# A shared expert's down products taken block by block, and 25 products that nobody reads at a scan's entry

## The chip, the cores and the metric

One NeuronCore of a Trainium2 chip runs the whole program in one launch. The metric is the device time of that launch in microseconds (us), the median over runs. Engines are called as the profile calls them: PE is TensorE (PEld its weight loads), DVE VectorE, ACT ScalarE, POOL GpSimd, SP the sync engine, whose queue (SPq) issues most DMAs.

## The reference, cut to what matters

16 sequences of 113 tokens (36 image patches and 77 text tokens) of width 256 go through an attention layer, a mixture-of-experts layer, a selective-scan (Mamba-like) layer and a fake-quantised gated FFN, each behind a layernorm and with a residual. The change touches the second and the entry of the third:

```python
# mixture of experts; x_ is (1808, 256)
idx = argmax(x_ @ router.T)                      # one of 8 experts for each token
y  = down_e( silu(x_ @ gate_e.T) * (x_ @ up_e.T) )          # by the chosen expert e
ys = silu(x_ @ w_gate_s.T) * (x_ @ w_up_s.T) @ w_down_s.T   # shared expert, 512 hidden units
out = y + ys
...
# selective scan; x = layernorm(h)
x_in, res = split(x @ in_proj_w.T + in_proj_b)
xc = silu(causal_conv4(x_in) + conv_b)
delta, Bp, Cp = split(xc @ x_proj_w.T + x_proj_b);  delta = softplus(delta @ dt_proj_w.T + dt_proj_b)
```

## The kernel before

Each engine has its own hand-written program; the order on an engine is the order of the code, and engines meet only by semaphores (`wait_ge`, `then_inc`). Loops (`Fori`) hold most repeated steps. PSUM is one tensor `ps` of 8 banks. Float32 products on PE show as two records each in the profile, bf16 products as one: 16 float32 products are "x32" there.

**Shared expert** (`pe_shared`, PE). Four groups of four sequences (452 tokens). In a group, for each of four blocks m of 128 hidden units, PE makes two gate and two up products (L1507) into banks 3 and 4 or 5 and 6. ACT takes the silu of the gate (L615), DVE multiplies it with up into `s_hT` block m (L1028, signals `sh_ready`). Then come the group's 16 down products (L1516): sequence by sequence, and within a sequence over the four blocks; the output of two sequences fills a bank (0 or 1), and `sdown_ps` tells DVE to add it to `resid` (L1032). All of them stand behind one wait for block 3. After the first block of group 0, `pe_counts` counts the router's choices (L1494, L1495). DVE turns them into slots, and POOL scatters all tokens into `slots_in` in DRAM, sorted by expert, with 16 indirect DMAs (L514).

**The experts' opening turns** (`pe_first_turns`, L1531). When the scatter is done, SP loads the first two tiles of 128 sorted tokens (`load_tile`, L390), and PE transposes them (four products, into banks 2 and 7). This stands in group 3, ahead of the gate and up products of its last block:

```python
            group(3, between=(HT - 1, pe_first_turns))
```

**Experts** (`pe_experts`). 22 tiles: gate and up (L1547), turning of the hidden block (L1566), turning of the tile two ahead (L1538), down (L1559). SP issues the loads of tile 2 and later only behind `sp.wait_ge(sdown_ps, 8)`, the last down product of the shared expert, and behind the loads of the scan's weights into the place of the shared expert's weights (`sh_w`), since all are on one queue. SP issues the FFN's gate and up weights right behind tiles 0 and 1.

**Scan entry** (`pe_ssm`, PE). After the last expert tile, DVE quantises a weight, PE turns it (L1610), ACT copies it (L665, `wqT_ready`); the experts' answers are gathered by DMA, DVE adds them to `resid` and takes statistics for sequences 0 and 1, then normalises these into `xn3` (L1226). PE turns them (`turn`, L1670), projects (`project_in`, L1680, two halves of 8 records), convolves (`convolve`, L1690), projects again (`project_x`, L1699; `project_dt`, L1706). ACT stands between: x3T (L718), pads (L729), silus (L740, L745) with a table load before and after, then `act_rstd` for the other 14 sequences (L544, L546), the projections (L754, L756) and softplus (L763 on). DVE adds the answers of those 14 sequences meanwhile (L1210, L1212) and works out their variance (L853), on which L544 waits. Then `step(0)` of the scan begins.

Of the kernel before, what the change touches and what calls it, by code (L numbers as in the profile page):

```python
# [17 lines left out]
P = 128  # L18
B, IMG, TXT, D = 16, 36, 77, 256
# [11 lines left out]
HT = HID // P  # L31
# [5 lines left out]
UP, GATE, DOWN, EW = 0, KT * HID, 2 * KT * HID, 2 * KT * HID + HT * D  # L37
# [15 lines left out]
AT_NORMALISE, AT_TURN, AT_IN, AT_PAD = 4, 5, 6, 7  # L53
OPENING = 1
AT_SKIP = (3, 4)
FIRST_SEQS, OTHER_SEQS = slice(0, GB), slice(GB, B)
BUT_ONE_SEQS, ONE_SEQ = slice(0, B - 1), slice(B - 1, B)
ROUTER_BANKS = (0, 1, 3, 4)
# [40 lines left out]
def build(nc, a, out):  # L99
    ctx = ExitStack()  # L100
    with ctx:
        def sb(name, shape, dt=F32):
            return ctx.enter_context(nc.sbuf_tensor(name, shape, dt))

        def sem(name):
            return ctx.enter_context(nc.semaphore(name))

        ps = ctx.enter_context(nc.psum_tensor("ps", [P, 8, 512], F32))
# [74 lines left out]
        sh_w = sb("sh_w", [P, EW])  # L183
# [66 lines left out]
        pick = pl.take((32 * P // 2,), 96).bitcast(BF16).rearrange("p (j m) -> p j m", j=32)  # L250
# [71 lines left out]
        sgate_ps, sup_ps, sgate_ready, sh_ready = sem("sgate_ps"), sem("sup_ps"), sem("sgate_ready"), sem("sh_ready")  # L322
        sdown_ps, sresid_ready = sem("sdown_ps"), sem("sresid_ready")
# [1166 lines left out]
        def pe_counts(pe):  # L1490

            pe.wait_ge(chosen_ready, 1)
            flat = chosenb[:, :, :].rearrange("p b e -> p (b e)")
            pe.matmul(ps[0:S, 2, 0:B * EXPERTS], upperb[:, :], flat, start=True, stop=True).then_inc(counts_ps, 1)  # L1494
            pe.matmul(ps[0:S, 7, 0:B * EXPERTS], onesb[:, :], flat, start=True, stop=True).then_inc(counts_ps, 1)  # L1495

        def pe_shared(pe):
            pe.wait_ge(xT2_ready, B)
            def group(g, between=None):
                for m in range(HT):  # L1500
                    if between is not None and between[0] == m:
                        between[1](pe)
                    par = m % 2
                    pe.wait_ge(sh_ready, g * HT + m + 1)
                    for bank, at, done in ((3 + 2 * par, GATE, sgate_ps), (4 + 2 * par, UP, sup_ps)):
                        for k in range(KT):
                            last = pe.matmul(ps[:, bank, 0:4 * S], sh_w[:, at + k * HID + m * P:at + k * HID + (m + 1) * P],  # L1507
                                             xT2[:, k, bass.ds(g * 4 * S, 4 * S)], start=k == 0, stop=k == KT - 1)
                        last.then_inc(done, 1)
                pe.wait_ge(sh_ready, g * HT + HT + 2)  # L1510
                for pair in range(2):
                    pe.wait_ge(sresid_ready, 2 * g + pair + 1)
                    for r in range(2):
                        for m in range(HT):
                            b = 2 * pair + r
                            last = pe.matmul(ps[0:S, pair, r * D:(r + 1) * D], s_hT[:, m, b * S:(b + 1) * S],  # L1516
                                             sh_w[:, DOWN + m * D:DOWN + (m + 1) * D], start=m == 0, stop=m == HT - 1,
                                             skip_group_check=True)
                    last.then_inc(sdown_ps, 1)

            group(0, between=(1, pe_counts))
            with pe.Fori(1, 3) as g:
                group(g)
            group(3, between=(HT - 1, pe_first_turns))

        def pe_first_turns(pe):
            pe.wait_ge(slots_ready, 1)
            for j, bank in enumerate(FIRST_TURNS):
                pe.wait_ge(xg_in[j], 16)
                for k in range(KT):  # L1530
                    last = pe.transpose(ps[:, bank, k * ETILE:(k + 1) * ETILE], xg[j][:, k * P:(k + 1) * P], ident)  # L1531
                last.then_inc(xgT_ps, 1)
# [128 lines left out]
                last.then_inc(fdown_ps, 1)  # L1661

        def pe_ssm(pe):
            def turn(g, first=False):
                pe.wait_ge(xn3_ready, GB * g + GB)
                if not first:
                    pe.wait_ge(proj_ready, 4 * g)
                for k in range(KT):
                    for r in range(GB):
                        last = pe.transpose(ps[:, 0, k * N + r * S:k * N + (r + 1) * S], xn3[r][:, k * P:(k + 1) * P], ident[0:S, 0:S])  # L1670
                last.then_inc(x3T_ps, 1)

            def project_in(g, par, half, first=False):

                pe.wait_ge(x3T_ready, g + 1)
                if not first:
                    pe.wait_ge(softplus_ready, g)
                for m in range(half * KT, half * KT + KT):
                    for k in range(KT):
                        last = pe.matmul(ps[:, 1 - m // KT, m % KT * N:(m % KT + 1) * N], in_w[:, k, m * P:(m + 1) * P], x3T[par][:, k, :],  # L1680
                                         start=k == 0, stop=k == KT - 1, skip_group_check=True)
                    if m % KT == KT - 1:
                        last.then_inc((xin_ps, res_ps)[m // KT], 1)

            def convolve(g):

                pe.wait_ge(xpad_ready, KT * g + KT)
                for m in range(KT):
                    for t in range(TAPS):
                        last = pe.matmul(ps[:, 1, m * N:(m + 1) * N], conv_diag[:, m, t, :], xpad[:, m, :, t:t + S],  # L1690
                                         start=t == 0, stop=t == TAPS - 1, skip_group_check=True)
                last.then_inc(conv_ps, 1)

            def project_x(g, par):
                pe.wait_ge(xc_ready, KT * g + KT)
                pe.wait_ge(res_ready, KT * g + KT)
                for w, rows, at in ((rank_w, RANK, 0), (bc_w, 96, N)):
                    for k in range(KT):
                        last = pe.matmul(ps[0:rows, 0, at:at + N], w[:, k, :], xc[par][:, k, :], start=k == 0, stop=k == KT - 1,  # L1699
                                         skip_group_check=True)  # L1700
                last.then_inc(proj_ps, 1)

            def project_dt(g):
                pe.wait_ge(proj_ready, 4 * g + 1)
                for m in range(KT):
                    last = pe.matmul(ps[:, 1, m * N:(m + 1) * N], dt_w[:, m * P:(m + 1) * P], rankT, start=True, stop=True, skip_group_check=True)  # L1706
                last.then_inc(dt_ps, 1)
# [31 lines left out]
            def skip(g, par, r):  # L1739
                if r == 0:  # L1740
                    pe.matmul(ps[0:S, 7, 0:GB * D].rearrange("p (b d) -> p b d", b=GB), ones2[:, 0:S],
                              outskip_b.unsqueeze(1).broadcast_to([2, GB, D]), start=True, stop=False, skip_group_check=True)
                for k in range(KT):
                    pe.matmul(ps[0:S, 7, r * D:(r + 1) * D], x3T[par][:, k, r * S:(r + 1) * S], skip_w[:, k, :], start=False,
                              stop=False, skip_group_check=True)
# [9 lines left out]
            def step(g, par, more=True, before=True, turn_next=True):  # L1755
                for c in range(CHUNKS):
# [22 lines left out]
                    if more and c == AT_RANK:  # L1779
                        project_x(g + 1, 1 - par)  # L1780
                    if c in AT_SKIP:
                        if before:
                            pe.wait_ge(resid3_ready, g)
                        skip(g, par, AT_SKIP.index(c))

            pe.wait_ge(diag_done, KT * (TAPS + 1))
            pe.wait_ge(pick_done, 1)
            pe.wait_ge(wqT_ready, 2 + 2 * FT + FT // 2)
            turn(0, first=True)
            for half in range(2):  # L1790
                project_in(0, 0, half, first=True)
            convolve(0)
            project_x(0, 0)
            project_dt(0)
            turn(1)
            spread(0, 0, 0)
            step(0, 0, before=False)
# [9 lines left out]
        @block.tensor  # L1807
        def _(pe):
            pe_tokens(pe)
            pe_attention(pe)  # L1810
            pe_router(pe)
            pe_shared(pe)
            pe_experts(pe)
            pe_weights_down(pe)
            pe_ssm(pe)
            pe_ffn(pe)
# [81 lines left out]
```

## Time and profile before

| | |
|---|---|
| time, median of 3 runs | 817.71 us (815.85 to 823.74) |
| the profiled execution | 817.4 us, its span 815.5 us |
| busy share of the span | PE 83%, PEld 56%, DVE 62%, ACT 47%, POOL 42% |
| mean granted clock of PE | 0.911 of 2.4 GHz |

The span runs from the first to the last instruction of the profile; 1.9 us lie around it. Times of rows count from the span's start. A granted clock of 1.00 is 2.4 GHz, one of 0.50 is 1.2 GHz. The stages that matter here: the shared expert from 205.6 to 293.5 us, the experts to 432.7, the scan's entry to about 463, the scan itself to about 745.

### The profile page before, as it was taken

What the parts mean: (1) busy time and instruction counts of PE and PEld (TensorE: products, weight loads), DVE (VectorE), ACT (ScalarE), POOL (GpSimd) and SP (SyncE); (2) the same over time, 40 slices, a digit from 0 to 9 for tenths busy, and PEclk for the clock granted to TensorE, in tenths of its full rate; (3) what the DMA queues carried; (4) which work ended last, traced back from release to release, by engine and by line L of the source; (5) the groups of instructions that cost most, each with busy time, mean ns of one, the idle gap of its engine ahead of it and who ended that gap; (6) DMA issues with size and microseconds to landing.
All of it is one profiled execution on the core that took longest, in us unless ns stands there. A gap on an engine that the chain in (4) does not pass through costs nothing. (4 is left out here: it accounts for less than half of the span.)

```text
span 815.5 us, 11659 instructions
## 1 busy us (share of the span) xinstructions
PE 677.0 (83%) x3648; PEld 453.4 (56%) x3649; DVE 503.9 (62%) x899; ACT 380.6 (47%) x843; POOL 345.5 (42%) x328
## 2 busy tenths in 40 slices
PE   7599999998999879999994878797887886733886
PEld 5478888876555446666663655455454552301444
DVE  1556666665412114444215768988988988995687
ACT  0366666763322103233222665665755755211965
POOL 0011211110357203232231168878879789540336
PEclk9899999997999998999997799999999997856799
DMA  9993000000021331111114201202202202000003
GB/s 243 311 426 126 0 0 0 0 2 1 5 41 27 113 107 40 46 41 50 40 39 105 92 31 62 92 2 92 92 0 92 92 1 92 1 0 0 1 1 92
DMA packets 28837, 52.89 MB, mean 65 GB/s; under 512 B 10976, under 2 KB 23684, under 8 KB 26628
## 3 DMA queue, kind: packets, MB, share of 16 engines
q1 hardware_dynamic: 20067, 47.62, 17.3%
q0 software_dynamic: 8736, 4.85, 2.4%
q8 instruction: 18, 0.29, 0.1%
q14 instruction: 16, 0.12, 0.0%
HBM read 42.75 MB, written 9.60 MB: 64 GB/s over the span
## 5 line engine op out<-in xcount | busy, mean ns | idle before, releaser
L483 POOL TENSOR_TENSOR arena<-arena 128x904 f32<-128x904 f32 x64 | 124.7, 1952 | 59.3 <-DVE arena L1251 53.0
L1251 DVE TENSOR_TENSOR_SCAN arena<-ps,arena 128x452 f32<-128x452 f32 x128 | 133.5, 1085 | 6.7 <-ACT ps L777 2.1
L777 ACT ACTIVATE ps<-arena,sh_w 128x448 f32<-128x448 f32 x128 | 80.3, 635 | 107.7 <-DVE arena L1251 106.8
L1730 PE MATMUL ps<-arena,const 128*128 128x452 f32 x112 | 63.3, 650 | 41.2 <-POOL arena L487 41.2
L1547 PE MATMUL ps<-arena,work 128*128 x176 | 83.5, 599 | 0.0
L557 ACT ACTIVATE work<-ps,work 113x113 f32<-113x113 f32 x256 | 66.8, 387 | 32.2 <-DVE work L908 32.2
L1241 DVE TENSOR_TENSOR arena<-arena,ps 128x904 f32<-128x904 f32 x64 | 69.2, 1082 | 11.0 <-PE ps L1717 10.8
L431 POOL TENSOR_TENSOR xT<-work 128x452 f32<-128x452 f32 x16 | 15.1, 944 | 142.2 <-DVE work L897 142.2
L530 POOL DMA_INDIRECT answers_e<-work,slot_token x22 | 23.7, 1075 | 110.0 <-DVE work L1046 110.0
L487 POOL TENSOR_TENSOR arena<-arena 128x452 f32<-128x452 f32 x56 | 64.0, 1143 | 4.4
L514 POOL DMA_INDIRECT slots_in<-xn,slot x16 | 37.9, 2366 | 56.0 <-issue 56.0
L1507 PE MATMUL ps<-xT,sh_w 128*128 128x452 f32 (+1 forms) x128 | 53.0, 572 | 0.0
L1730 PEld LDWEIGHTS ps<-arena,const 128*128 128x128 f32 x112 | 19.2, 207 | 53.2 <-POOL arena L487 53.1
L1042 DVE TENSOR_TENSOR work<-ps,work 128x512 f32<-128x512 f32 x22 | 15.2, 691 | 52.2 <-PE ps L1547 52.2
L1559 PE MATMUL ps<-arena,work 128*128 x176 | 43.5, 391 | 0.8 <-ACT work L628 0.8
L1547 PEld LDWEIGHTS ps<-arena,work 128*128 128x128 f32 x176 | 31.2, 192 | 22.9 <-issue 22.3
L908 DVE TENSOR_REDUCE work<-ps 113x4 f32<-113x452 f32 x64 | 35.8, 621 | 11.5 <-PE ps L1378 11.5
L1507 PEld LDWEIGHTS ps<-xT,sh_w 128*128 128x128 f32 x128 | 25.6, 202 | 24.0 <-issue 23.6
L1680 PE MATMUL ps<-arena,sh_w 128*128 128x226 f32 x128 | 37.9, 457 | 0.7 <-ACT arena L718 0.7
L1357 PE MATMUL ps<-work 128*128 128x113 f32 x256 | 35.6, 297 | 2.3 <-ACT work L551 1.7
L624 ACT ACTIVATE work<-ps 128x512 f32<-128x512 f32 x22 | 13.1, 597 | 52.3 <-PE ps L1547 52.3
L615 ACT ACTIVATE work<-ps 128x452 f32<-128x452 f32 x16 | 8.8, 548 | 60.3 <-PE ps L1507 60.3
(243 smaller groups left out, 1394.6 us busy)
## 6 DMA issues: line engine op xcount, KB each, us to landing
arena<-c_rows SPq DMA_DIRECT2D x8, 1808.0 KB, 6.4
arena<-in_ex_w SPq DMA_DIRECT2D x8, 1536.0 KB, 23.9
slots_in<-work SPq DMA_DIRECT2D x1, 2827.0 KB, 23.5
work<-slots_in SPq DMA_DIRECT2D x22, 128.5 KB, 2.0
xn<-answers_e SPq DMA_DIRECT2D x4, 448.0 KB
out<-resid SPq DMA_DIRECT2D x8, 224.0 KB
arena<-in_patches SPq DMA_DIRECT2D x3, 576.0 KB, 6.3
sh_w<-in_sh_w SPq DMA_DIRECT2D x1, 1536.0 KB, 11.5
```

What stands on the lines that cost most here:

```text
L483: pool.tensor_tensor(read[kp], state[kp], c_all[par][:, 2 * c:2 * c + 2, :].unsqueeze(2).broadcast_to([P, 2, KT, N]), ALU.mult)\
L487: pool.tensor_tensor(read[kp][:, 0], read[kp][:, 0], read[kp][:, 1], ALU.add).then_inc(pair_ready, 1)
L514: pool.indirect_dma_start(slots_in, bass.IndirectOffsetOnAxis(ap=slot[:, b:b + 1], axis=0), xn2_named[:, b, :], None).then_inc(scattered, 16)
L557: last = act.activation(probs[:, r, j], ps[0:S, 3 + r, j * S:(j + 1) * S], ACT.Exp, bias=negmax[:, h:h + 1])
L777: act.activation(decay_ps(n)[:, :, 1:], delta[par].rearrange("p k (b s) -> p (k b) s", b=GB)[:, :, 1:], ACT.Exp, scale=a_neg[:, 2 * c + n: ...
L1241: dve.tensor_tensor(drive[kp], dx[par].unsqueeze(1).broadcast_to([P, 2, KT, N]), ps[:, 2 + kp, 0:2 * N].rearrange("p (n s) -> p n s", n=2) ...
L1251: dve.tensor_tensor_scan(state[kp][:, n].rearrange("p k s -> p (k s)"), decay_ps(n).rearrange("p q s -> p (q s)"), drive[kp][:, n].rearran ...
L1507: last = pe.matmul(ps[:, bank, 0:4 * S], sh_w[:, at + k * HID + m * P:at + k * HID + (m + 1) * P], xT2[:, k, bass.ds(g * 4 * S, 4 * S)], s ...
L1547: last = pe.matmul(ps[:, bank, :], xgT[par][:, k, :], arena[:, bass.ds(e * EW + at + k * HID, HID)], start=k == 0, stop=k == KT - 1)
L1559: last = pe.matmul(ps[:, 6, 0:D], e_hT[:, m, :], arena[:, bass.ds(e * EW + DOWN + m * D, D)], start=m == 0, stop=m == HT - 1)
L1680: last = pe.matmul(ps[:, 1 - m // KT, m % KT * N:(m % KT + 1) * N], in_w[:, k, m * P:(m + 1) * P], x3T[par][:, k, :], start=k == 0, stop=k ...
L1730: pe.matmul(ps[:, 6, 0:KT * N], ident, read[kp][:, 0].rearrange("p k s -> p (k s)"), start=False, stop=False, skip_group_check=True).then_ ...
```

## The change

In the shared expert's groups the loop over blocks m is now the outer one of the down products: the products of block 0 for all four sequences, then block 1, and so on, each block behind its own wait for `sh_ready`, so that only block 3's products wait for block 3. Four sums are open at once, in four regions of banks 0 and 1; `start` is set on the first product of each bank alone. Both `sdown_ps` signals come within the last block. The opening turns go from before the last block of gate and up products to before the last block of down products in group 3. At the scan's entry PE gets `stay_busy(n)`: n bf16 products of 128 x 384 into bank 7, which nobody reads: 19 ahead of the first turn, 2 behind it, 4 behind the convolution.

```diff
+FILL = (19, 2, 4)
...
         def pe_shared(pe):
             pe.wait_ge(xT2_ready, B)
-            def group(g, between=None):
+            def group(g, counts=False, turns=False):
                 for m in range(HT):
-                    if between is not None and between[0] == m:
-                        between[1](pe)
+                    if counts and m == 1:
+                        pe_counts(pe)
...
-                pe.wait_ge(sh_ready, g * HT + HT + 2)
-                for pair in range(2):
-                    pe.wait_ge(sresid_ready, 2 * g + pair + 1)
-                    for r in range(2):
-                        for m in range(HT):
+                for m in range(HT):
+                    if turns and m == HT - 1:
+                        pe_first_turns(pe)
+                    pe.wait_ge(sh_ready, g * HT + m + 3)
+                    for pair in range(2):
+                        if m == 0:
+                            pe.wait_ge(sresid_ready, 2 * g + pair + 1)
+                        for r in range(2):
                             b = 2 * pair + r
                             last = pe.matmul(ps[0:S, pair, r * D:(r + 1) * D], s_hT[:, m, b * S:(b + 1) * S],
-                                             sh_w[:, DOWN + m * D:DOWN + (m + 1) * D], start=m == 0, stop=m == HT - 1,
+                                             sh_w[:, DOWN + m * D:DOWN + (m + 1) * D], start=m == 0 and r == 0, stop=m == HT - 1,
                                              skip_group_check=True)
-                    last.then_inc(sdown_ps, 1)
-
-            group(0, between=(1, pe_counts))
+                        if m == HT - 1:
+                            last.then_inc(sdown_ps, 1)
+
+            group(0, counts=True)
             with pe.Fori(1, 3) as g:
                 group(g)
-            group(3, between=(HT - 1, pe_first_turns))
+            group(3, turns=True)
...
         def pe_ssm(pe):
+            def stay_busy(products):
+                for _ in range(products):
+                    pe.matmul(ps[:, 7, 0:3 * P], pick[:, 0, :], pick[:, 0:3, :], start=True, stop=True)
...
             pe.wait_ge(wqT_ready, 2 + 2 * FT + FT // 2)
+            stay_busy(FILL[0])
             turn(0, first=True)
+            stay_busy(FILL[1])
             for half in range(2):
                 project_in(0, 0, half, first=True)
             convolve(0)
+            stay_busy(FILL[2])
             project_x(0, 0)
```

How PE's program moves in the last group of the shared expert. Before (L1507 gate and up, L1531 the opening turns, L1516 down):

```order
127 L1507 MATMUL ps<-xT,sh_w 128x452 x12
128 L1531 MATMUL ps<-const,work 128x128 x4
129 L1507 MATMUL ps<-xT,sh_w 128x452 x4
130 L1516 MATMUL ps<-sh_w,work 113x256 x16
131 L1570 TENSOR_LOAD tile_expert
```

After, where L1508 is gate and up, L1536 the turns, L1520 down:

```order
130 L1508 MATMUL ps<-xT,sh_w 128x452 x16
131 L1520 MATMUL ps<-sh_w,work 113x256 x12
132 L1536 MATMUL ps<-const,work 128x128 x4
133 L1520 MATMUL ps<-sh_w,work 113x256 x4
134 L1575 TENSOR_LOAD tile_expert
```

The turns have moved behind four more gate and up products and twelve down products (one row is one product here, not one record).

PE's program at the scan's entry, before (L1610 the last weight's turns, L1670 turn, L1680 project_in, L1690 convolve, L1699 project_x, L1706 project_dt):

```order
408 L1610 MATMUL ps<-const,work 64x128 x2
409 L1670 MATMUL ps<-const,arena 128x113 x4
410 L1680 MATMUL ps<-arena,sh_w 128x226 x8
411 L1690 MATMUL ps<-arena,xT 128x226 x8
412 L1699 MATMUL ps<-arena,sh_w 64x226 x2
413 L1699 MATMUL ps<-arena,sh_w 96x226 x2
414 L1706 MATMUL ps<-arena,sh_w 128x226 x2
```

After (L1671 the products nobody reads, L1679 turn, L1689 project_in, L1699 convolve, L1708 project_x):

```order
411 L1615 MATMUL ps<-const,work 64x128 x2
412 L1671 MATMUL ps<-xT 128x384 x19
413 L1679 MATMUL ps<-const,arena 128x113 x4
414 L1671 MATMUL ps<-xT 128x384 x2
415 L1689 MATMUL ps<-arena,sh_w 128x226 x8
416 L1699 MATMUL ps<-arena,xT 128x226 x8
417 L1671 MATMUL ps<-xT 128x384 x4
418 L1708 MATMUL ps<-arena,sh_w 64x226 x2
```

Nothing else moves on PE, and no instruction of another engine changes.

## Rows read from the trace of the kernel before

**Rows 1.** Windows: stretch in us, length, busy of each engine, PEclk, DMA share, GB/s.

```profile
313.00:432.00 119.00, 118.21 (x468) 73.41 (x467) 45.37 (x112) 34.19 (x72) 35.79 (x79) 1.00 0.14 43
...
281.00:283.00 2.00, 2.00 (x4) 0.81 (x3) 0.00 (x0) 0.00 (x0) 0.60 (x3) 0.50 1.01 332
440.00:445.00 5.00, 0.00 (x0) 0.00 (x0) 3.41 (x17) 1.95 (x4) 0.00 (x0) 0.50 0.99 239
448.00:450.00 2.00, 2.00 (x7) 1.76 (x7) 1.90 (x7) 0.00 (x0) 0.00 (x0) 0.50 0.00 0
```

**Rows 2.** Timeline of PE, shared expert: start us, us, what [idle before <-releaser].

```profile
220.65 7.16 PE L1516 MATMUL ps<-sh_w,work 128*113 128x256 f32 x32 [0.79 <-DVE work L1028]
227.64 12.30 PE L1507 MATMUL ps<-xT,sh_w 128*128 x32
240.81 7.16 PE L1516 MATMUL ps<-sh_w,work 128*113 128x256 f32 x32 [0.87 <-DVE work L1028]
...
267.97 9.26 PE L1507 MATMUL ps<-xT,sh_w 128*128 128x452 f32 x24
280.20 0.81 PE L1531 MATMUL ps<-const,work 128*128 128x128 f32 x4 [2.96 <-DMA work<-slots_in]
280.80 4.88 PE L1507 MATMUL ps<-xT,sh_w 128*128 128x452 f32 x8
286.47 7.16 PE L1516 MATMUL ps<-sh_w,work 128*113 128x256 f32 x32 [0.79 <-DVE work L1028]
293.46 5.31 PE L1547 MATMUL ps<-arena,work 128*128 x12
...
306.74 0.69 PE L1538 MATMUL ps<-const,work 128*128 128x128 f32 x2 [5.80 <-DMA work<-slots_in]
```

**Rows 3.** Instructions of line L1507: duration ns min/median/max, first and last start.

```profile
L1507 PE MATMUL ps<-xT,sh_w x128: 542/542/1059, 205.6 to 285.1; 128*128 128x452 f32 x64, 128*128 x64
```

**Rows 4.** Timeline of SP's queue, from the first tile load to the third.

```profile
278.02 0.80 SPq L390 DMA_DIRECT2D work<-slots_in  x2
...
293.66 0.35 SPq L400 DMA_DIRECT2D sh_w<-in_in_w  x1
...
301.82 24.22 SPq L390 DMA_DIRECT2D work<-slots_in  x5
```

**Rows 5.** Timeline of all engines at the scan's entry.

```profile
439.61 0.65 ACT L665 ACTIVATE dq<-ps 128x256 bf16<-128x256 f32 x2 [0.20 <-PE ps L1610]
...
445.49 0.98 PE L1670 MATMUL ps<-const,arena 113*128 113x113 f32 x4 [5.91 <-DVE arena L1226]
...
447.17 5.41 PE L1680 MATMUL ps<-arena,sh_w 128*128 128x226 f32 x16 [0.70 <-ACT arena L718]
...
452.41 3.22 PE L1690 MATMUL ps<-arena,xT 128*128 128x226 f32 x16
...
455.67 0.79 ACT L745 ACTIVATE arena<-ps,sh_w 128x226 f32<-128x226 f32 x2 [2.19 <-PE ps L1690]
...
456.51 1.92 PE L1699 MATMUL ps<-arena,sh_w 128*64 128x226 f32 x8 [0.88 <-ACT arena L745]
...
457.16 0.17 DVE L853 SCALAR_TENSOR_TENSOR lnt<-lnt 113x14 f32<-113x14 f32 x1
...
457.77 0.21 ACT L544 ACTIVATE lnt<-lnt 113x14 f32<-113x14 f32 x1
...
458.46 0.45 ACT L754 ACTIVATE arena<-ps,sh_w 64x226 f32<-64x226 f32 x1 [0.23 <-PE ps L1699]
...
460.02 0.79 ACT L763 ACTIVATE arena<-ps,sh_w 128x226 f32<-128x226 f32 x2
460.04 0.58 PE L1670 MATMUL ps<-const,arena 113*128 113x113 f32 x4
```

**Rows 6.** Timeline: the second convolution, in the scan's first step.

```profile
471.97 4.96 PE L1690 MATMUL ps<-arena,xT 128*128 128x226 f32 x16 [2.65 <-ACT arena L729]
```

**Rows 7.** Timeline of PE: products that nobody reads, in the FFN stage, as they stand before.

```profile
783.47 2.47 PE L1616 MATMUL ps<-arena,identb 128*128 128x452 bf16 x12 [1.70 <-DVE arena L1151]
```

## The prediction

> **What bounds the kernel now.** I read the page first (PE busy for 83% of the span), then windows by stage, then the timelines of the two places that the change touches, and the chain of waits for what follows them. In the experts' stage PE is busy for 118.2 of 119 us at full clock [rows 1]: PE alone sets its length, so whatever time it starts earlier it ends earlier, provided that its data come earlier too. Ahead of it lies the shared expert, also PE's: in PE's timeline [rows 2] the reader is to see two kinds of holes. Each group's down products wait for DVE's product of block 3 (0.79 to 0.87 us), and the opening turns wait 2.96 us for the tiles that SP loads when the scatter is done. Behind that second hole the eight gate and up records from 280.80 take 4.88 us, while 24 of them took 9.26 before: the granted clock is 0.50 from 281 to 283 [rows 1], the 1.2 GHz level, after PE stood still for 3 us. At the scan's entry PE stands for 5.91 us until DVE has normalised the first two sequences [rows 5], with the clock at 0.50 through the wait and into the projections [rows 1].
>
> **The waits for block 3.** How much do they cost from start to start? Group 1: down at 220.65, gate and up at 227.64, down at 240.81. The 32 gate and up records take 12.30 us, the last of them 0.54 [rows 3], so 31 steps take 11.76, a step 0.379 and 32 steps 12.14; from 227.64 to 240.81 are 13.17, so 1.03 us are lost. Group 2 repeats it (1.03); in groups 0 and 3 the idle row is 0.79 in place of 0.87, so 0.95 each. Together 3.96 us. In the new order the first down products need block 0, whose `s_hT` was ready three blocks ago, and block 3's products come after 24 records at (227.64 - 220.65) / 32 = 0.218 us, 5.2 us; block 3 was late by 1 us. No new wait takes the place of the old. The three more waits in a group are on counts long reached: nothing. `sdown_ps` of the first pair comes 2 us or more later than before, but DVE then has over 5 us until the next group's first product, and PE asks for the sums (`sresid_ready`) 12 us later: hidden. Gain 3.96.
>
> **The opening turns.** PE's start of group 3 comes earlier by the three waits before it, 3.0 us: 264.95. Then 32 gate and up records, 12.14, to 277.1, and 24 down records, 5.2, to 282.3. The tiles were there at 280.1: the scatter hangs on the router's counts in group 0 (unchanged place) and on its own DMAs, and SP issues the loads at 278.02 [rows 4], so this time stays. PE arrives 2.2 us after them and waits for nothing. What goes: the hole, from the due next start (267.97 + 9.26 - 0.54 + 0.38 = 277.07) to 280.20, 3.13 us; and the low clock behind it: seven steps from 280.80 to the last start at 285.14 take 4.34 in place of 7 x 0.379 = 2.65, so 1.69; the turns themselves, 0.2 or nothing, I take 0.1. Gain 4.9. Is ACT late with the copies of the turned tiles? They are due at 284.6, when PE begins the experts; the turns end at 282.8 and eight down records (1.75) still stand between: no.
>
> Sum: 3.96 + 4.9 = 8.9 us at the end of the shared expert, 293.46 to about 284.6. **Does it stay?** The next hole is at 306.74, where PE waits 5.80 us for tile 2 [rows 2]. That load does not hang on the scatter: SP gets past its wait for the last down product at 293.66, issues sixteen loads of scan weights, reaches tile 2 at 301.82, and it lands by 306.7 [rows 4]. So this chain, 13.3 us, starts with PE's last down product and moves with it. The FFN weights that SP issues right behind tiles 0 and 1 (1.57 MB) fill the DMA engines (share 1.01 at 332 GB/s from 281 to 283, [rows 1]); at that rate they take 4.7 us and end by 285 or 286, and scan weights will now be issued from 284.8. They overlap by 1.5 us at most: the cost is between nothing and 1.5. I take nothing, since SP spends eight us on issuing the scan weights, time enough for what is left over to drain. Then the experts' stage moves whole.
>
> **The scan's entry.** The 19 products start when ACT's last weight copy is done, 440.3 [rows 5], and the turn's data come at 445.4: 5.1 us to fill. Twelve of the FFN's bf16 products of 452 columns take 2.47 us [rows 7], less the last's 0.35 that is 0.193 a step, 0.164 for 384 columns at full clock and twice that, 0.33, at the low one. So 19 take 3.1 us (all full) to 6.2 (all low): end between 443.4 and 446.5, against 445.4. As the projections rose to full clock some 4 us after PE began at 447.17, a switch midway is likely, and the fill ends within half a us of the data. Gain from the clock: the turn takes 0.58 in place of 0.98, and 16 records of projection 3.22 (the convolution's pace) in place of 5.41 [rows 5]: 0.4 + 2.2 = 2.6 us for PE, less at most 1.1 if the fill overruns. The two products behind the turn (0.3) lie in a wait of 0.70, the four behind the convolution (0.65) in one of 0.88.
>
> But **what is late next?** After its silus ACT must do `act_rstd` for the other 14 sequences, which needs DVE's L853, done at 457.33; before, L544 began at 457.77, just when the table load after the silus was done. DVE's chain of additions does not feel PE's clock. So L544 comes 0.4 earlier, no more. L754 then waits no longer for the projection (0.23), which makes 0.6. But PE, done at some 456, stands for over 2 us until L754, and the clock may fall there again: then project_dt (four records) takes 0.7 longer and L763, at 460.02 before, gains nothing. Of 2.6 us between -0.2 and 0.6 come through; I take 0.4.
>
> **Sum.** 3.96 + 4.9 + 0.4 = 9.3 us from a profiled 817.4, whose span was 815.5. The profiled execution stands 0.3 below the median, so from 817.7: 808.4.
>
> **A rule that speaks against it.** The down products before filled one region of one bank at a time; now every pair of records goes to another of four regions in two banks. The trace shows the gate and up products switching banks every four records at an even 0.379 step and a granted clock of 1.00. The Trainium skill (TensorE: Matmul & The Clock Gate, section "A second HAM failure mode: psum-queue depth-cycling") tells of a kernel whose cycling through PSUM banks left small gaps in PE's work, so that its clock swung between the levels. No run here shows that yet; it is the mechanism of the last rival below.
>
> **The rivals.**
> (a) *The clock is kinder than in this profile.* In the scan's first step the convolution [rows 6] takes 4.96 us, 1.74 over its full-clock 3.22, and the chain of waits runs through it. With PE's work shifted, the clock may stand high there: 817.7 - 9.3 - 1.7 = 806.7. For it: here the fall came just as that convolution began. Against: the median holds other executions with other luck. Chance 0.13.
> (b) *Part is given back between 285 and 320 us*: the overlap of weight loads delays tile 2 by 1.5, or the clock is low for one more stretch of 1.7 behind that wait (it falls there already). 9.3 - 1.6 = 7.7: 810.0. With both, 811.6. Chance 0.17.
> (c) *The fill overruns*, at the low clock all through: the turn is 1.1 late, and the projections cold as before. The silus then end 1.1 later, with the table load behind them, and L544 begins at 458.9 instead of 457.77. 8.9 - 1.1 = 7.8: 809.9. Chance 0.08.
> (d) *The change does not do what it says*: the shared expert ends earlier, but tile 2 does not come earlier (the queue's transfers, not PE, set it), and PE's wait at 306.74 grows by what was won. Then only the entry counts: 817.3. Against it stands that SP issued nothing from 280 to 293.66. Chance 0.07.
> (e) *Slower*: the down products, cycling over two banks, leave gaps, and the clock falls in them. At the low level a record takes 0.22 us more. 42 of the 128 records at the low level eat 9.3 us; from there on it is slower. With all 128, 28 us: 817.7 - 9.3 + 28 = 836. Chance 0.05.
>
> **How the numbers follow.** The forecast has 0.50: 808.4, by itself 806.5 to 810.5, since the entry's term is worth 0.6 at most and runs of the same kernel differ by a few us. The bound that a measurement can tell, 1%, is 8.2 us here: faster means below 809.5. Of the forecast three quarters lie below it, 0.38, with (a) 0.13 and parts of (b) and (c), 0.07: 0.58. Slower is (e), 0.05 (all of it taken over 1%). The rest, 0.37, is the same. The range 805.0 to 812.0 holds the forecast, (a), (b) and (c), 0.88 by name and some 0.8 with what I have not thought of.
>
> **What the profile after would show.** Right, if: no idle row over 0.3 us stands ahead of L1520, the turns (L1536) have no wait for a DMA, granted clock 1.00 from 212 to 300; the experts' first products (L1552) start at 284 to 285; the wait for tile 2 is again 5 to 6 us, and its load is issued 8 us after the last down product; the fill's 19 products end within 1 us of the turn, project_in takes 3.3 to 4 us; L544 directly follows L853, and L763 stands no more than 0.7 us nearer to the entry's start than before. Wrong, if: the tiles land later than PE's arrival, tile 2's wait grows, down records take over 0.22 a step, or the entry gives all 2.6 us, which would mean that ACT's wait for DVE was not the bound.

## The result, and the profile after

The changed kernel takes 807.91 us (median of 4 runs, 804.52 to 809.96), the kernel before beside it 816.78 (4 runs, 815.21 to 823.74): a ratio of 0.9872, 95% interval 0.9835 to 0.9908, so 8.9 us less. The forecast was 808.4, its range 805.0 to 812.0. The same kernel measured once more (e11, below) took 810.26 beside 817.30, 7.0 us less, ratio 0.9908. The profiled execution of the changed kernel took 809.96 with a span of 808.2 and stands at the upper end of its runs, so between the two traces only 7.3 us of span are to be found, not 8.9.

PE's timeline of the shared expert, after (columns as in [rows 2]):

```profile
205.61 5.76 PE L1508 MATMUL ps<-xT,sh_w 128*128 128x452 f32 x8
211.21 0.22 PE L1495 MATMUL ps<-chosenb,upperb 113*113 113x128 bf16 x1
...
220.48 7.07 PE L1520 MATMUL ps<-sh_w,work 128*113 128x256 f32 x32
227.38 12.30 PE L1508 MATMUL ps<-xT,sh_w 128*128 x32
239.52 7.07 PE L1520 MATMUL ps<-sh_w,work 128*113 128x256 f32 x32
...
265.46 12.30 PE L1508 MATMUL ps<-xT,sh_w 128*128 128x452 f32 x32
277.60 5.34 PE L1520 MATMUL ps<-sh_w,work 128*113 128x256 f32 x24
282.78 0.60 PE L1536 MATMUL ps<-const,work 128*128 128x128 f32 x4
283.21 1.89 PE L1520 MATMUL ps<-sh_w,work 128*113 128x256 f32 x8
284.94 5.31 PE L1552 MATMUL ps<-arena,work 128*128 x12
...
298.45 0.69 PE L1543 MATMUL ps<-const,work 128*128 128x128 f32 x2 [6.04 <-DMA work<-slots_in]
```

No row from 220.48 to 284.94 has idle time in brackets: the waits for block 3 are gone. From 227.38 to 239.52 are 12.14 us: 32 steps of 0.379 and nothing else, where [rows 2] had 13.17. The turns stand inside the down products and wait for no DMA. The windows answer to [rows 1]: the stretch from 281 to 283, in which the granted clock was 0.50, is at 1.00.

```profile
212.00:284.00 72.00, 72.00 (x247) 44.80 (x246) 17.61 (x38) 17.87 (x24) 39.09 (x22) 1.00 0.20 40
281.00:283.00 2.00, 2.00 (x12) 1.62 (x12) 0.00 (x0) 0.00 (x0) 1.20 (x6) 1.00 0.54 148
```

SP's queue, after, answers to [rows 4]: from the first scan weight behind the last down product (285.13) to tile 2 (293.28) it takes 8.15 us, as before (293.66 to 301.82).

```profile
279.22 0.80 SPq L391 DMA_DIRECT2D work<-slots_in  x2
...
285.13 0.35 SPq L401 DMA_DIRECT2D sh_w<-in_in_w  x1
...
293.28 12.47 SPq L391 DMA_DIRECT2D work<-slots_in  x3
```

The scan's entry, all engines, after ([rows 5]):

```profile
432.10 5.10 PE L1671 MATMUL ps<-xT 96*128 96x384 bf16 x19 [0.83 <-ACT dq L666]
...
437.04 0.61 PE L1679 MATMUL ps<-const,arena 113*128 113x113 f32 x4
...
438.35 3.33 PE L1689 MATMUL ps<-arena,sh_w 128*128 128x226 f32 x16 [0.37 <-ACT arena L719]
...
448.80 0.17 DVE L854 SCALAR_TENSOR_TENSOR lnt<-lnt 113x14 f32<-113x14 f32 x1
...
449.01 0.21 ACT L545 ACTIVATE lnt<-lnt 113x14 f32<-113x14 f32 x1 [2.15 <-DVE lnt L854]
...
449.37 0.43 ACT L755 ACTIVATE arena<-ps,sh_w 64x226 f32<-64x226 f32 x1
...
449.86 1.87 PE L1715 MATMUL ps<-arena,sh_w 64*128 64x226 f32 x4 [2.33 <-ACT arena L755]
...
451.76 0.79 ACT L764 ACTIVATE arena<-ps,sh_w 128x226 f32<-128x226 f32 x2 [0.97 <-PE ps L1715]
...
454.55 0.63 DVE L1233 TENSOR_TENSOR arena<-arena 128x452 f32<-128x452 f32 x1 [2.86 <-issue]
```

PE's work is quick (16 records of projection in 3.33 us instead of 5.41), and then ACT waits 2.15 us for DVE's L854, PE waits 2.33 for ACT, and the four records of project_dt take 1.87 us, 0.47 each. The windows show why: the granted clock is 1.00 in the projections and 0.50 in project_dt, behind PE's wait.

```profile
438.00:440.00 2.00, 1.65 (x9) 1.64 (x10) 1.90 (x6) 0.30 (x1) 0.00 (x0) 1.00 0.02 4
450.00:452.00 2.00, 2.00 (x6) 1.36 (x7) 1.61 (x7) 1.03 (x4) 1.06 (x2) 0.50 0.05 11
```

Where the span's 7.3 us are, by the start of the same piece of work in the two traces:

```
place                                  before    after    gained so far
counts in group 0                      210.42    211.21      -0.79
first expert product                   293.46    284.94       8.52
turn of tile 2                         306.74    298.45       8.29
statistics of 14 sequences (L853/854)  457.16    448.80       8.36
first step of the scan (L1232/1233)    462.81    454.55       8.26
last 12 down products                  809.57    800.95       8.62
end of the span                        815.5     808.2        7.3
```

From the counts to the experts it is 83.04 before and 73.73 after: 9.31 us. This stretch is steady: in the traces of all nine kernels that have both edits of the shared expert it is 73.73 or 73.74. On the side of before it moves with the tiles: in e4, which has the old shared expert, it is 82.22, the tiles being issued 66.7 us after the counts instead of 67.6. So the two edits are worth 8.5 to 9.3 us.

Two losses hide 2 us of it in the span. Ahead of the counts, group 0's eight gate and up records took 5.76 us instead of 4.97. And the last twelve down products of the FFN, at the end of the kernel, took 3.21 us instead of 1.93, behind the same wait of 1 us. The change touches neither place.

```profile
800.95 3.21 PE L1665 MATMUL ps<-dq,work 128*113 128x256 bf16 x12 [0.99 <-ACT work L714]
```

Before, that row read:

```profile
809.57 1.93 PE L1660 MATMUL ps<-dq,work 128*113 128x256 bf16 x12 [0.99 <-ACT work L713]
```

### The profile page after: what moved, and what is told of

Read it like the earlier page. It is cut to its first block and busy times, and to the rows that moved or that the text cites. A ratio compares the mean times of both kernels' runs of the same rounds, so it can differ in the third digit from the quotient of the medians.

```text
span 808.2 us, 11710 instructions
## 1 busy us (share of the span) xinstructions
PE 681.7 (84%) x3673; PEld 456.9 (57%) x3674; DVE 504.1 (62%) x899; ACT 380.9 (47%) x843; POOL 345.7 (43%) x328
## 5 line engine op out<-in xcount | busy, mean ns | idle before, releaser
L1508 PE MATMUL ps<-xT,sh_w 128*128 128x452 f32 (+1 forms) x128 | 51.9, 565 | 0.0
L1552 PEld LDWEIGHTS ps<-arena,work 128*128 128x128 f32 x176 | 31.2, 192 | 22.7 <-issue 22.1
L1508 PEld LDWEIGHTS ps<-xT,sh_w 128*128 128x128 f32 x128 | 25.3, 199 | 23.9 <-issue 23.5
L1564 PEld LDWEIGHTS ps<-arena,work 128*128 128x128 f32 x176 | 32.9, 197 | 5.3 <-issue 1.5
L1689 PE MATMUL ps<-arena,sh_w 128*128 128x226 f32 x128 | 34.7, 425 | 0.9 <-ACT arena L719 0.9
L1385 PE MATMUL ps<-const,work 113*113 113x113 f32 x256 | 33.7, 264 | 1.7 <-ACT work L558 1.7
```

The source lines that it names most:

```text
L1552: last = pe.matmul(ps[:, bank, :], xgT[par][:, k, :], arena[:, bass.ds(e * EW + at + k * HID, HID)], start=k == 0, stop=k == KT - 1)
L1564: last = pe.matmul(ps[:, 6, 0:D], e_hT[:, m, :], arena[:, bass.ds(e * EW + DOWN + m * D, D)], start=m == 0, stop=m == HT - 1)
```

## The experiments

Each table line of a run is its median, the lowest and highest time, and the ratio to the kernel before, timed on the same chip, with the 95% interval. "From the counts" is the time from the counts to the first expert product.

### The parts by themselves

**e1_down_only**: the new order of the down products, with the turns where they stood and no fill.

```diff
-FILL = (19, 2, 4)
+FILL = (0, 0, 0)
@@ gate and up loop
+                    if turns and m == HT - 1:
+                        pe_first_turns(pe)
@@ down loop
-                    if turns and m == HT - 1:
-                        pe_first_turns(pe)
```

> Down products by block of units alone: the opening turns stay ahead of the last block of gate and up products, and there are no products that nobody reads. My theory: the parts do not add. The waits for block 3 go in all four groups (4.0 us), but PE then comes to the turns 3.0 us earlier while the tiles land at the same time, so the wait for the tiles grows from 3.0 to about 6.0 us and swallows the first three; the low clock behind it stays. Only group 3's own wait (0.95) is won: the ratio to before is 0.998 to 1.000, and the shared expert ends near 292.5. The rival (each part stands for itself): 4 us less, ratio 0.995.

Measured: 819.11 us (816.29 to 822.54, 12 runs), ratio 0.9994 (0.9968 to 1.0020). From the counts: 82.52, 0.5 less than before. PE's timeline shows where the gain of the three groups went:

```profile
266.94 9.26 PE L1510 MATMUL ps<-xT,sh_w 128*128 128x452 f32 x24
...
282.34 1.14 PE L1536 MATMUL ps<-const,work 128*128 128x128 f32 x4 [6.14 <-DMA work<-slots_in]
283.26 5.20 PE L1510 MATMUL ps<-xT,sh_w 128*128 128x452 f32 x8
```

Counted from the counts, PE arrives 3.3 us earlier at the turns and waits 3.2 us longer there: 6.14 instead of 2.96. The turns begin 69.7 us after the counts here and 69.8 before: the tiles come no sooner for it. So the waits for block 3 were real, and removing them alone was worth half a us.

**e3_turns_only**: the old order of the down products; the turns go from ahead of the last gate and up block to behind it.

```diff
                     last.then_inc(done, 1)
+                if between is not None and between[0] == HT:
+                    between[1](pe)
                 pe.wait_ge(sh_ready, g * HT + HT + 2)
@@
-            group(3, between=(HT - 1, pe_first_turns))
+            group(3, between=(HT, pe_first_turns))
```

> The turns alone are moved: to between the last gate and up products and the first down products of group 3, the down products in their old order, no products that nobody reads. My theory: PE reaches the turns at about 280.1, just as the tiles land; the hole of 3.1 us and the low clock behind it (1.7) go, and the turns cover most of the wait for block 3 (0.6): 5.2 us less, ratio 0.9935. With the first run's 1 us this makes 6 us, under the 8.9 of both together. The rival (the low clock is not of this hole): 3.1 to 3.7 us less, the products after the turns at 0.22 us a record only in part.

Measured: 812.62 us (808.04 to 815.31, 6 runs), ratio 0.9913 (0.9883 to 0.9944). From the counts: 77.63, 5.41 less.

```profile
265.56 12.30 PE L1507 MATMUL ps<-xT,sh_w 128*128 128x452 f32 x32
277.69 0.60 PE L1533 MATMUL ps<-const,work 128*128 128x128 f32 x4
278.64 7.16 PE L1518 MATMUL ps<-sh_w,work 128*113 128x256 f32 x32 [0.35 <-DVE work L1028]
```

No wait for the tiles, no low clock behind one, and the turns even cover 0.5 us of the wait for block 3. In this trace the tiles were issued 66.1 us after the counts instead of 67.6; PE, 69.7 us after the counts, would have waited about nothing at 67.6 too, since a tile lands some 2 us after its issue.

**e2_shared_only**: the changed kernel without the fill.

```diff
-FILL = (19, 2, 4)
+FILL = (0, 0, 0)
```

> Both edits of the shared expert, none of the 25 products. My theory: 8.5 to 9 us less than before, ratio 0.989, and no more than 0.6 us more than with the 25 products, since ACT's wait for DVE's statistics of the other 14 sequences absorbs what a fast PE wins at the scan's entry; L544's row follows the table load as before. The rival (the clock at the entry is worth its 2.6 us): 2 to 3 us slower than with the 25 products.

Measured: 809.69 us (808.25 to 810.73, 6 runs), ratio 0.9872 (0.9844 to 0.9900). From the counts 73.73, as with the whole change. The parts do not add: 0.5 from the down order and 5.4 from the turns make 5.9, both together 9.3. Of the missing 3.4 us, 3.2 are the longer wait of e1. Without the fill the time is as short as with it, at the same ratio of 0.9872.

**e4_fill_only**: the kernel before with the 25 products that nobody reads.

```diff
+            stay_busy(19)
             turn(0, first=True)
+            stay_busy(2)
             for half in range(2):
                 project_in(0, 0, half, first=True)
             convolve(0)
+            stay_busy(4)
```

> The 25 products alone, on the kernel before. My theory: 0 to 0.6 us, ratio 0.999 to 1.000, though PE's turn, projection and convolution end 2.2 to 2.6 us earlier after the answers' statistics: L544 starts right behind L853, and PE stands longer ahead of project_dt, which runs at the low clock. The rival: 2.6 us less, ratio 0.997.

Measured: 817.64 us (815.99 to 820.81, 12 runs), ratio 0.9982 (0.9960 to 1.0004): no change that can be told, a gain of 3.3 us at most. At the entry:

```profile
454.84 0.17 DVE L853 SCALAR_TENSOR_TENSOR lnt<-lnt 113x14 f32<-113x14 f32 x1
...
455.90 1.03 PE L1710 MATMUL ps<-arena,sh_w 64*128 64x226 f32 x4 [2.33 <-ACT arena L754]
...
459.74 0.63 DVE L1232 TENSOR_TENSOR arena<-arena 128x452 f32<-128x452 f32 x1 [2.01 <-issue]
```

Here project_dt ran at full clock behind the same wait of 2.33 us. From the statistics to the first step of the scan are 4.90 us, against 5.65 before and 5.75 in the changed kernel: 0.75 gained in this execution, 0.1 lost in that one, and the 0.84 between them are project_dt (1.03 and 1.87). Executions without the fill differ by 0.3 at this place themselves: 5.65 before, 5.68 in e1, 5.39 in e2, 5.38 in e3.

### The entry: what holds it

**e5_fill_dt**: the changed kernel with 13 more products in PE's wait ahead of project_dt.

```diff
             project_x(0, 0)
+            stay_busy(13)
             project_dt(0)
```

> The changed kernel with 13 more products that nobody reads, between project_x and project_dt at the scan's entry. In the changed kernel PE stood 2.33 us there and project_dt ran at the low clock (1.87 us in place of 1.03). My theory: 13 x 0.164 = 2.1 us fill the wait, project_dt is back at 1.03 and softplus starts 0.8 us earlier after the statistics (L854): 0.8 us less than the changed kernel, ratio to before 0.9865. The rival (the low clock there costs nothing, since ACT is busy with the projections until then): no change.

Measured: 810.04 us (807.6 to 815.49, 10 runs), ratio 0.9910 (0.9873 to 0.9947). In its trace project_dt took 1.03 and the stretch 4.90 us, as in e4. The 0.8 us that were expected cannot be seen in the time, its interval being 6 us wide.

**e6_rstd_later** and **e7_rstd_later_nofill**: ACT takes the 14 other sequences' statistics after the projections, so that it does not wait for DVE in between; e6 is the changed kernel with this edit, e7 the same without the fill.

```diff
-            act_rstd(act, 4, OTHER_SEQS, load=False)
             projections(0, 0, first=True)
+            act_rstd(act, 4, OTHER_SEQS, load=False)
```

> The changed kernel with ACT's act_rstd for the 14 other sequences moved from ahead of the projections to behind them. My theory: ACT's wait for DVE's statistics was what absorbed the clock's gain; with the projections ahead of it ACT fills that wait, softplus starts at about the statistics' end + 0.6 instead of + 2.9, and DVE's steps(0) start some 2.2 us earlier: ratio to before 0.9850 to 0.9860. The rival (something else, c rows or PE, holds the first step): under 1 us.

> As the run before, without the 25 products. My theory: here PE at the low clock ends project_x only about a microsecond after the statistics, so the projections come as late as before and the statistics' Ln and Exp stand behind them: 0.3 us slower than with both edits of the shared expert alone, and 2.5 us slower than the run before: only with the two edits together does the entry give its 2.6 us. Ratio to before 0.9885 to 0.9895. The rival: the order on ACT alone gives the gain, and the two runs are equal.

Measured: e6 808.12 us (803.42 to 811.66, 6 runs), ratio 0.9859 (0.9808 to 0.9910); e7 810.81 (807.29 to 811.3, 6 runs), 0.9894 (0.9849 to 0.9939). The entry of e6:

```profile
445.22 0.44 ACT L755 ACTIVATE arena<-ps,sh_w 64x226 f32<-64x226 f32 x1 [0.70 <-PE ps L1708]
...
445.72 1.03 PE L1715 MATMUL ps<-arena,sh_w 64*128 64x226 f32 x4 [0.53 <-ACT arena L755]
...
446.46 0.17 DVE L854 SCALAR_TENSOR_TENSOR lnt<-lnt 113x14 f32<-113x14 f32 x1
...
446.67 0.21 ACT L545 ACTIVATE lnt<-lnt 113x14 f32<-113x14 f32 x1
...
449.93 0.63 DVE L1233 TENSOR_TENSOR arena<-arena 128x452 f32<-128x452 f32 x1
```

ACT no longer waits for the statistics, project_dt follows at once at full clock, and from the statistics to the scan are 3.47 us; in e7, with PE cold at the turn, 5.73. In e2, without the fill and in ACT's old order, they are 5.39. So in the traces neither edit alone wins anything, and both together win 2 us: it is ACT's wait for DVE that swallowed the fill. The medians point the same way (2.7 us between e6 and e7), but their intervals overlap, and e6 at 0.9859 cannot be told from the changed kernel (0.9872 and 0.9908): in time this is not shown.

### The next wait

**e8_tile2_early**: SP loads tiles 2 and 3 ahead of its wait for the last down products, and so ahead of the scan's weights.

```diff
+            load_tile(2, 0, False)
+            load_tile(3, 1, False)
             sp.wait_ge(sdown_ps, 8)
...
-            with sp.Fori(0, (ETILES - 2) // 2) as i:
+            with sp.Fori(1, (ETILES - 2) // 2) as i:
```

> The changed kernel with SP's loads of tiles 2 and 3 ahead of its wait for the shared expert's last down product, so also ahead of the scan weights. My theory: tile 2's load hung on that wait and on sixteen issues (8 us), not on the tiles or the DMA engines; it now lands before 290, and PE's wait of 6.0 us ahead of tile 2's turn goes, with the low clock behind it. What is late next is ACT, which waits for the scan weights (a_neg) between tiles 0 and 1 and loads two tables: down of tile 1 comes 5 us earlier instead of 7.7. 5 to 6 us less than the changed kernel, ratio to before 0.981. The rival (ACT's wait for the scan weights takes its place whole): under 1 us less.

Measured: 803.41 us (801.75 to 807.42, 6 runs), ratio 0.9826 (0.9780 to 0.9872). The turn of tile 2 has no wait now. PE's hole is smaller and behind another load, ACT's, as the rows from 288 to 303 of PE and ACT show:

```profile
288.35 0.38 PE L1545 MATMUL ps<-const,work 128*128 128x128 f32 x2
...
294.23 0.22 ACT L649 ACTIVATE sh_w<-sh_w 128x16 f32<-128x16 f32 x1 [3.78 <-DMA sh_w<-in_a_log]
294.46 1.28 ACT L627 ACT_TABLE_LOAD   x1
...
296.99 2.77 PE L1566 MATMUL ps<-arena,work 128*128 x8 [2.45 <-ACT work L631]
299.56 2.83 PE L1554 MATMUL ps<-arena,work 128*128 x4
```

ACT waits 3.78 us for `in_a_log`, the last of the sixteen loads behind SP's wait, to take an exponential that the scan needs much later; it is followed by a table load, and PE stands for 2.45 us and then works more slowly (2.77 us for eight records that take 1.89, 2.83 for four that take 1.88).

The edit is worth less than the 5 to 6 us that were expected: from the experts' first product to the first of the 19 products are 143.44 us, against 147.16 in the changed kernel, 3.7 less.

**e9_rstd_tile2**: e6 and e8 together.

> Two edits together on the changed kernel: ACT's act_rstd behind the projections, and SP's loads of tiles 2 and 3 ahead of its wait for the last down product. They lie in different stages with PE fully busy between, so they should add: 5.3 to 6 us and 2.2 us less than the changed kernel, ratio to before 0.979. The rival (one takes the other's room): not under 0.981.

Measured: 803.62 us (801.96 to 804.82, 6 runs), ratio 0.9827 (0.9792 to 0.9861). The median missed what was expected (0.979) and equals that of e8; its interval is too wide to say whether e6's edit adds anything. PE's timeline of the profiled execution shows where e6's gain at the entry was lost in it:

```profile
426.98 3.25 PE L1673 MATMUL ps<-xT 96*128 96x384 bf16 x19 [0.82 <-ACT dq L668]
431.45 0.61 PE L1681 MATMUL ps<-const,arena 113*128 113x113 f32 x4 [1.23 <-DVE arena L1229]
432.76 5.01 PE L1691 MATMUL ps<-arena,sh_w 128*128 128x226 f32 x16 [0.37 <-ACT arena L721]
```

The same 19 products ran at full clock from the first one on, took 3.25 us instead of 5.10, and ended 1.23 us before the turn's data. Behind this stand the granted clock fell (1.00 from 430 to 432, 0.50 from 434 to 436), and the projection took 5.01 us. From the statistics to the scan are 5.15 us, where e6 had 3.47.

An early end of the fill is not enough for this. In e8 the 19 products ended just as early, and the projection ran at full pace:

```profile
428.97 0.60 PE L1681 MATMUL ps<-const,arena 113*128 113x113 f32 x4 [1.25 <-DVE arena L1229]
...
430.27 3.33 PE L1691 MATMUL ps<-arena,sh_w 128*128 128x226 f32 x16 [0.37 <-ACT arena L721]
```

So did it in e5 and e6, with stands of 0.81 and 1.03 us. What decides between the two outcomes was not examined.

**e10_aneg_later**: e9, and ACT takes the exponential of `in_a_log` one tile later.

```diff
-                if j == 0:
+                if j == 1:
                     act.wait_ge(ssm_in, 16 * 15)
```

> As the run before, and ACT takes the exponential of a_neg one tile later. With the tile loads early, ACT waited 3.78 us for a_neg's load, with a table load before and after, and PE stood 2.45 us and fell to the low clock. My theory: one tile later the data are there, only the two table loads (2.6 us) stay, in ACT's slack of some 4 us a tile: 2.5 to 4 us less than the run before, ratio 0.975. The rival (DVE's tables now wait for ACT and hold the next tile's product): no gain.

Measured: 798.66 us (797.62 to 801.15, 6 runs), ratio 0.9772 (0.9737 to 0.9807): 5.0 us below e9 on the same chip, more than the 2.5 to 4 expected, and faster than both kernels. ACT does the same work without a wait, and PE has no hole in this stage:

```profile
298.23 1.28 ACT L649 ACT_TABLE_LOAD   x1
299.52 0.22 ACT L649 ACTIVATE sh_w<-sh_w 128x16 f32<-128x16 f32 x1
299.75 1.28 ACT L627 ACT_TABLE_LOAD   x1
301.27 0.60 ACT L627 ACTIVATE work<-ps 128x512 f32<-128x512 f32 x1 [0.23 <-PE ps L1554]
```

The stage from the experts' first product to the 19 products is 139.07 us, 4.7 less than the 143.74 of e9, where PE stood for 2.71 us and lost 1.8 more in slow records behind it. At the entry the fill, 5.64 us long this time, ended 1.1 us after the turn's data; from the statistics to the scan are 4.50 us.

**e11_after_again**: the changed kernel once more, beside e9 and e10.

> The changed kernel once more, as the base for the two runs beside it. From the traces so far its gain is 8.5 us ahead of the scan and nothing at the entry: ratio to before 0.9875 to 0.9895.

Measured: 810.26 us (805.85 to 812.35, 8 runs), ratio 0.9908 (0.9875 to 0.9941). The two measurements of the changed kernel, 0.9872 and 0.9908, lie about as far apart (2.9 us) as anything that the fill could do; the change as a whole is faster in both. On this chip e10 with its three further edits is 11.6 us below it.

## The prediction, point by point

**The waits for block 3** (3.96 us). Right in size: 12.14 instead of 13.17 us from start to start, and no idle row is left. A down step became 0.2156 us (6.90/32, from 220.48 to 227.38) where it was 0.2184, which over 128 records is 0.36 more that the sum did not have; why it is shorter was not examined. That the gain comes through only because the turns move too was not said there; e1 shows it.

**The turns** (4.9 us). Right: PE comes to them 71.6 us after the counts, the tiles at some 70, and neither hole nor low clock is left; e3 alone shows 5.41 us. Predicted start of the experts 284.6, found 284.94, with group 0's 0.79 in it. Together 9.31 us from the counts on, for 8.9 forecast and 0.36 of the down step.

**Does it stay?** Right. The wait for tile 2 is 6.04 instead of 5.80 us. Of the overlap that the prediction put at "between nothing and 1.5" these 0.24 cannot be told from chance: the wait is 5.45 in e11, the same kernel, and 6.86 in e4, with the old shared expert. That the chain runs through SP's queue behind the last down product, e8 shows: with the load issued ahead of it the wait is gone. Rival (d) falls, and of rival (b) nothing is seen that is clear of this spread. One sign was set too far: the granted clock was to be 1.00 from 212 to 300, but the wait for tile 2 now ends at 298.45, and behind it the eight down records of the expert take 3.62 us, as they did before at 307.22. That fall had moved ahead of 300 with everything else.

**The entry** (0.4 us). The mechanism is right: the fill ends with the turn's data (437.2 against 437.04), the turn takes 0.61, the projections 3.33, L545 follows L854 directly (0.21 instead of 0.61 behind it), ACT's copy comes 0.33 sooner after that. The step that was left open, project_dt at the low clock, happened in the profiled execution and took all of it back: 5.75 against 5.65 us, -0.1. In e4 and e5 it did not, and 0.75 came through. What the fill is worth in time cannot be told: e4 against the kernel before is 0.9982 with 1.0 just inside its interval, e2 without the fill is as fast as the whole. Rival (c), the fill that overruns, did not come in this execution; in e11, the same kernel, the fill ended 0.3 us after the turn's data and in e10 1.1, with the projections at full pace (3.33) in both. That ACT's wait for DVE was the bound is shown by the traces of e2, e6 and e7.

**The other rivals.** (a), the kinder clock in the scan's first convolution, was 4.74 instead of 4.96: no. (e), the slower one, did not come. The granted clock is 1.00 from 212 to 284 and the down step got shorter, not longer. What the Trainium skill tells of another kernel (TensorE: Matmul & The Clock Gate, "A second HAM failure mode: psum-queue depth-cycling"), a clock that swings because of small gaps as the work cycles through PSUM banks, did not occur in this pattern of four regions in two banks, at 0.216 us a record.

**Not foreseen.** Span against span, the forecast was 9.3 us and the two profiled executions show 7.3. The two places that the change does not touch, 0.79 in group 0 and 1.28 in the last twelve down products, are 2.07; the other differences (0.45 more from the counts to the experts, 0.5 less at the entry, some tenths elsewhere) about cancel. The first place is chance of the execution: e5 runs the same program up to the counts and took 4.93 us there. For the second this is less clear. All eight profiled executions of kernels with the fill show the low clock in the last down products, and only one of the five without it (e1; before, e2, e3 and e7 took 1.93). In e10 (6.54 us), and in e1, e4, e5 and e11 (6.58 each), it covers the last 24:

```profile
786.60 6.54 PE L1667 MATMUL ps<-dq,work 128*113 128x256 bf16 x24 [0.34 <-DVE arena L1185]
```

The same 24 took 4.82 us before, from 806.68 to 811.50. Some 350 us lie between the fill and this place, and no trace shows a link; whether the fill costs these 1.3 to 1.8 us stays open.

The median, 807.91, stands 0.5 us from the forecast, and that closeness is luck: its four runs spread over 5.4 us, the kernel before was 0.9 us faster beside it than the 817.7 from which the forecast counts, and e11 gave 810.26.

## What to carry to other kernels

A wait for data that come at a fixed time takes back whatever is won ahead of it: e1 won 3 us and waited 3.2 longer. Move the consumer of such data behind work that does not need them first, and then remove the small waits; here this order is worth 9.3 us and the parts by themselves 0.5 and 5.4. When a wait is gone, look for the next one on the same engine and ask what it really hangs on: two more, each a load or an early step standing ahead of something urgent in a queue (e8, e10), shortened the experts' stage by 3.7 and 4.7 us in the traces, and no engine had less work to do. To fill a wait so that the clock stays up pays only where the engine behind it does not wait for something else; and a fixed count of products lasts 3.25 or 5.1 to 5.6 us by the clock at its start, so it ends early in one execution and late in another.

## What the runs showed of the hardware

- The same 19 products of 384 columns took 3.25 us in e5, e6, e8 and e9, and 5.10 to 5.64 in e4, e10, e11 and the changed kernel, by the clock at their start. In the first case they ended 0.81 to 1.25 us early. Behind such a stand the projection took 3.33 us in three of the four executions and 5.01 in e9.
- The granted clock behind the same wait differs between executions: behind 2.33 us of standing, project_dt took 1.87 us in the changed kernel and 1.03 in e4; behind 1 us, the last twelve down products took 3.21 in the changed kernel and 1.93 before. A level that a trace shows behind a wait of this length is one case, not a price.
- SP issued the first tile loads 66.1 to 68.0 us after the router's counts, in executions of the same scatter, so 2 us of the distance between PE and the tiles are chance.
- Down products that go to another of four PSUM regions in two banks with every product kept PE's granted clock at 1.00 from 212 to 284 us, with a record started every 0.216 us.
